# GpSimd waits for the landing of a group of indirect transfers before it issues the next group, in four stages of a graph network

## What is computed

```python
# layer 0: gated edge messages, then a norm over the graph
msg = silu(h[src] + (edge_attr @ we.T + be)); agg = segment_sum(msg, dst)
# layer 1: one softmax over all edges, messages summed by src
e = leaky_relu(h[src] @ a_src + h[dst] @ a_dst + a_b); att = softmax(e, axis=0)
out = segment_sum(att * h[dst], src)
# layer 2: eight heads, softmax over the edges of a node
score = clip(K[src] . Q[dst] / 4, -5, 5); out = segment_sum(softmax_dst(score) * V[src], dst)
# layer 3: an MLP over [x[src], x[dst], edge_attr], summed by dst, then an MLP over nodes
rel = mlp(concat(x[src], x[dst], edge_attr)); out = mlp(concat(x, segment_sum(rel, dst)))
```

## Time and profile before

| | |
|---|---|
| median of 3 runs | 6226.86 us (6226.12 to 6229.10) |
| profiled execution, first to last instruction | 6321.6 us |
| busy: PE, DVE, ACT, POOL | 67%, 47%, 26%, 54% of the span |
| conv, GpSimd's first to last gather | 88.5 to 1351.4 us |
| place | 1514.7 to 2881.2 us |
| heads | 3237.0 to 4619.6 us |
| relation | 4691.2 to 6161.0 us |

### The profile page before, as it was taken

One profiled execution on the slowest core, in us unless ns is written; L12 is line 12 of the kernel. 1 busy time (PEld: TensorE's weight loads), 2 busy tenths in 40 slices (PEclk: granted clock), 3 DMA queues, 4 the chain that ended last, 5 costly groups with the idle time before them and its releaser, 6 DMA issues. The chain is left out here.

```text
span 6321.6 us, 91693 instructions
## 1 busy us (share of the span) xinstructions
PE 4256.0 (67%) x19917; PEld 3740.8 (59%) x19918; DVE 2983.7 (47%) x8050; ACT 1666.9 (26%) x2996; POOL 3424.5 (54%) x3536
## 2 busy tenths in 40 slices
PE   3555555556777777787855555555568888888887
PEld 3444544445766777776744445445456666667765
DVE  5444444456332333235755555555564444444445
ACT  0111111113222222226732222222233333333331
POOL 3655655532566656566635556555525555555550
PEclk6666566666555555558976666666679999998999
DMA  4233323234222222225733333333334444444441
GB/s 103 81 83 83 83 78 82 80 71 109 78 80 80 80 80 81 79 77 169 206 99 99 100 97 101 99 101 97 98 105 131 132 131 133 128 128 132 133 128 48
DMA packets 491156, 645.54 MB, mean 102 GB/s; under 512 B 94519, under 2 KB 354059, under 8 KB 490798
## 3 DMA queue, kind: packets, MB, share of 16 engines
q0 software_dynamic: 132032, 325.99, 18.1%
q1 hardware_dynamic: 346462, 312.02, 17.6%
q10 hardware_dynamic: 12560, 6.52, 0.6%
HBM read 554.38 MB, written 89.82 MB: 102 GB/s over the span
## 5 line engine op out<-in xcount | busy, mean ns | idle before, releaser
L1610 POOL DMA_INDIRECT R<-table_ps,r_idx x832 | 809.6, 973 | 731.9 <-DVE r_idx L1684 417.5
L1195 POOL DMA_INDIRECT by_src<-R,p_idx x832 | 826.3, 993 | 627.9 <-issue 246.0
L1390 POOL DMA_INDIRECT R<-table_kv,h_idx x832 | 805.3, 968 | 647.7 <-issue 324.3
L660 POOL DMA_INDIRECT R<-table,c_idx x784 | 750.5, 957 | 548.5 <-issue 307.7
L1420 PE MATMUL psum<-R,h_oh 128*128 128x137 f32 x1664 | 405.0, 415 | 627.8 <-issue 291.4
L693 PE MATMUL psum<-R,c_oh 128*128 x1664 | 380.1, 400 | 620.4 <-DVE R L752 375.0
L1420 PEld LDWEIGHTS psum<-R,h_oh 128*128 128x128 f32 x1664 | 344.2, 295 | 679.8 <-issue 494.5
L693 PEld LDWEIGHTS psum<-R,c_oh 128*128 128x128 f32 x1664 | 324.3, 290 | 673.5 <-issue 673.5
L1632 PE MATMUL psum<-w_L_gnn_re_w,r_ea 128*128 128x256 f32 x1664 | 555.3, 417 | 226.5 <-DVE X L1724 209.7
L1745 DVE TENSOR_TENSOR R<-R,psum 128x256 f32 x832 | 346.9, 417 | 752.0 <-remote 344.6
L1008 PE MATMUL psum<-R 128*128 x1664 | 428.5, 424 | 189.0 <-issue 187.0
(11 more groups left out here) (339 smaller groups left out, 7696.9 us busy)
## 6 DMA issues: line engine op xcount, KB each, us to landing
R<-by_src SPq DMA_DIRECT2D x220, 260.0 KB, 3.1
r_ea<-in_ea_t SPq DMA_DIRECT2D x832, 64.0 KB
R<-in_ea_t SPq DMA_DIRECT2D x196, 256.0 KB
R<-rel_rows SPq DMA_DIRECT2D x104, 256.0 KB
R<-lo_rows SPq DMA_DIRECT2D x104, 256.0 KB
h_rel<-rel_rows SPq DMA_DIRECT2D x208, 128.0 KB
r_rel<-rel_rows SPq DMA_DIRECT2D x208, 128.0 KB
by_src<-R,p_idx POOLq DMA_INDIRECT x832
```

Source lines behind the costliest of these rows:

```text
L660: g.indirect_dma_start(out=rows[:, u, :], out_offset=None, in_=table, in_offset=bass.IndirectOffsetOnAxis(ap=idx[:, j // GROUPS % 2, u:u + ...
L1195: g.indirect_dma_start(out=by_src, out_offset=bass.IndirectOffsetOnAxis(ap=idx[:, u:u + 1], axis=0), in_=rows[:, u, :], in_offset=None).th ...
L1390: g.indirect_dma_start(out=rows[:, u, :], out_offset=None, in_=table, in_offset=bass.IndirectOffsetOnAxis(ap=idx[:, u:u + 1], axis=0)).the ...
L1610: g.indirect_dma_start(out=rows[:, u, :], out_offset=None, in_=table, in_offset=bass.IndirectOffsetOnAxis(ap=idx[:, u:u + 1], axis=0)).the ...
```

## The change

GpSimd gets one more wait before it begins a group of four transfers: for the semaphore of the last transfer of the preceding group. In conv this holds for every group but the very first; in place, heads and relation for the second, third and fourth group of each iteration (`if u:`), not for the first. In conv the first 16 groups are now written out ahead of the loop (`loads=PER`), so that the loop runs 11 rounds. Nothing else is changed: the same transfers, slots and waits of the other engines.

```diff
--- before.py
+++ after.py
@@ -654,6 +654,10 @@
                     if j % GROUPS == 0:
                         g.wait_ge(idx_ready, TURNS * i + j // GROUPS + 1)
                     g.wait_ge(row_free, PER * i + j + 1)
+                    if not (isinstance(i, int) and i == 0 and j == 0):
+                        before_j = (j - 1) % GROUPS
+                        turn = TURNS * i + j // GROUPS + (1 if j % GROUPS else 0)
+                        g.wait_ge(row_in[G * before_j + G - 1], 16 * turn)
                     g.sem_inc(pool_turn, 1)
                     for q in range(G):
                         u = G * (j % GROUPS) + q
@@ -661,7 +665,7 @@
                                              in_offset=bass.IndirectOffsetOnAxis(ap=idx[:, j // GROUPS % 2, u:u + 1], axis=0)
                                              ).then_inc(row_in[u], 16)
 
-                staggered(g, PER, (gather, 0, TILE_GROUPS))
+                staggered(g, PER, (gather, 0, TILE_GROUPS), loads=PER)
 
             @block.tensor
             def _(pe):
@@ -1191,6 +1195,8 @@
                             g.wait_ge(ready, n + 1)
                         if u % G == 0:
                             g.wait_ge(rows_ready, 2 * n + u % G8 // G + 1 + 2 * PER)
+                            if u:
+                                g.wait_ge(row_out[u - 1], 16 * i + 16)
                             g.sem_inc(pool_turn, 1)
                         g.indirect_dma_start(out=by_src, out_offset=bass.IndirectOffsetOnAxis(ap=idx[:, u:u + 1], axis=0),
                                              in_=rows[:, u, :], in_offset=None).then_inc(row_out[u], 16)
@@ -1386,6 +1392,8 @@
                         if u % G == 0:
                             g.wait_ge(idx_ready, GROUPS * i + u // G + 1)
                             g.wait_ge(msg_ready, GROUPS * i + u // G + 1)
+                            if u:
+                                g.wait_ge(row_in[u - 1], 16 * i + 16 * (before + 1))
                             g.sem_inc(pool_turn, 1)
                         g.indirect_dma_start(out=rows[:, u, :], out_offset=None, in_=table,
                                              in_offset=bass.IndirectOffsetOnAxis(ap=idx[:, u:u + 1], axis=0)
```

## The result

The changed kernel takes **6829.75 us** (median of four runs, 6828.59 to 6839.71) against 6226.49 (6223.87 to 6229.10): a ratio of 1.0965 [1.0941, 1.0990], or +603 us. The forecast was +343, and the time lies above the range. The sign is as predicted, and so is conv as the stage that loses most; the size is not.

What follows compares the result with a forecast made beforehand. No engine is full; GpSimd runs groups ahead, held by VectorE, except in place. Conv +158, heads +59, relation +20 and place +110 make +347 us profiled, scaled to +342: 6570 us, range 6390 to 6740.

Steps and rivals of the forecast that it cites:

- the cushion: GpSimd's present idle time per group boundary: 1.72 us in conv, 1.70 in place, 1.88 in heads, 2.29 in relation.
- The restart: At each waited boundary, GpSimd begins 0.84 us after its release, as read from VectorE's message in the timeline.
- The landing: Last packets of each stage's last transfer begin 2.8 us after issue in conv, 1.8 place, 3.1 heads, 3.2 relation.
- Conv: Gap 2.6 us at 195 boundaries, group 7.33 us against 6.45, GpSimd becomes the bound: +158 us.
- Place: Gap 2.1 us, iteration 26.1 against 26.3, but boundaries without lead make ScalarE late: +110 us, between none and 179.
- Heads: Gap 2.8 us at three of four boundaries, iteration 27.8 us against 26.6: +59 us.
- The base: Terms summed on the profiled 6321.6 us, 1.5% above the median 6226.86, then scaled in proportion: +347 becomes +342 us.
- Relation: Gap 2.8 us, iteration 27.9 against 28.3, fits on average; scattering iterations cost +20 us, bounded by 0 and 130.
- The long gap: Rival: gap 3.1 us in all stages and place pays in full, 6907 us; chance 0.12.
- The short gap: Rival: gap 2.1 us in all stages, conv +60, place +60, heads and relation fit, 6347 us; chance 0.10.
- The wait is met: Rival: thresholds count too low, the wait is met when reached, nothing changes, 6227 us; chance 0.02.
- the level case: Rival: gap 1.7 us everywhere, GpSimd stays ahead in conv, 6215 to 6240 us; chance 0.04.

Runs made afterwards that it cites:

- e11: Wait in conv alone, SyncE's load held back until GpSimd begins its next group, against the kernel before: 6486.17 us, ratio 1.0199.
- e2: The new wait in place alone, the other stages as before, against the kernel before: 6366.35 us, ratio 1.0231.
- e13: The three waits in place alone, SyncE's loads there tied to GpSimd's groups, against the kernel before: 6234.04 us, ratio 1.0019.
- e14: The waits in heads alone, SyncE's load per group there tied to a group's start, against the kernel before: 6348.28 us, ratio 1.0189.
- e4: The new wait in relation alone, the other stages as before, against the kernel before: 6201.84 us, ratio 0.9974.
- e7: Wait in conv alone, but for the last gather of the group two back, against the kernel before: 5154.30 us, ratio 1.0004.
- e9: The whole change run again in the third session, against the kernel before (6365.78 us there): 6834.44 us, ratio 1.0736.
- e15: The whole change run again in the fourth session, against the kernel before (6224.20 us there): 6816.44 us, ratio 1.0940.
- e12: Wait in place alone, only the one between the halves of an iteration, against the kernel before: 6351.16 us, ratio 0.9974.

## Why the prediction was right in sign and wrong in size

**What bounds the kernel, and the cushion.** Right: GpSimd became the bound in conv and heads as forecast, and the cushion of 1.7 to 2.3 us per boundary, summed over an iteration, is what the gaps had to exceed. It did so in place too, where the forecast took the floor (26.1) to be level with the pace.

**The restart, 0.84 us.** About right: 0.76 us in conv and relation, 0.79 in place and 0.86 in heads, from the rise of the semaphore to the next transfer.

**The landing: the step that failed.** The prediction read it from "the last transfer of each stage, behind which nothing is queued". That is one landing per stage, and not in the case that the change makes the rule. The wait puts the readers, and through their buffers SyncE's loads, in step with the landing, so that in conv and at two of three boundaries in place a 256 KB load nearly always runs beside the very transfer that is waited for. Measured landings are 3.0 us in conv (2.8 taken, by when packets begin; another 0.35 until the semaphore is seen to rise was left out) and 3.4, 1.9 and 3.0 in place (1.8 taken, and the gap raised to 2.1). Moving the loads brings place's gap to 2.23, so its 2.1 was a good figure for an undisturbed scatter. Conv's 2.6 was not: an undisturbed gather gives 2.4. The gather that it was read from was itself a slow one. The packets that raise its semaphore are 4 bytes each and don't show in the slices; the last of them began 4.0 us after the issue, against 2.2 us for those of e11. So a single last transfer was no measure either way. The three terms:

- *Conv*, 2.6 forecast, 3.2 measured: 195 x 0.6 = 117 us. The message after runs from 96.2 to 1643.6, before from 96.0 to 1367.1: +276, which is the forecast's 158 and this 117.

```profile
L756 DVE TENSOR_TENSOR R<-psum,R x196: 680/692/693, 96.2 to 1643.6; 128x512 f32<-128x512 f32 x196
its engine sat idle before it (us, times) until:
  DMA R<-table,c_idx: 389.5, 185
```

- *Place*, 2.1 forecast, 3.16 measured: the floor of an iteration rises to 29.3 us, three above today's, and the stage pays 3.0 x 52 = 156 (e2: +144 in time). The +110 rested on another ground, boundaries without slack that make ScalarE late. ScalarE does wait for scatters now, 1015.9 us in 89 waits where it had 423.3 on what the profile calls remote; but that is GpSimd being the bound seen from ScalarE: in e13 it still waits for scatters for 668.2 us in 65 waits, and the time is up by 12 us only.

```profile
ACT R L1051 <- DMA by_src<-R,p_idx: 1015.9, 89, 13.4
```

- *Heads*, 2.8 forecast. The waits view of GpSimd lists all three boundaries of each iteration, after and then in e14:

```profile
POOL R L1398 <- DMA R<-table_kv,h_idx: 452.0, 156, 4.1
```

```profile
POOL R L1395 <- DMA R<-table_kv,h_idx: 410.5, 156, 3.4
```

  452.0 / 156 = 2.90 us, and 2.63 with the loads moved. Some 20 us for the gap; the transfers also keep GpSimd for 999 ns instead of 968, 832 x 0.031 = 26 us, which the forecast held constant.

**The base.** The sum was made against the profiled execution and scaled by 0.985 as a whole. That execution was slow mainly in heads (26.6 us per iteration; 25.3 to 25.7 in four traces of the same code where before takes 6226 us) and a little in conv. With GpSimd as the bound a stage's end doesn't depend on how slow it was before, so the cost of the wait has to be counted from the median's pace: some 55 us more in heads, some 20 in conv. These terms against the misses: in conv 117 + 20 = 137 for 131, in heads 20 + 26 + 55 = 101 for 91, in place 156 - 110 = 46 for 36. They were found after the fact, and what is left is within the intervals of the single runs.

**Relation.** The gap is as forecast (2.78 and 2.8), and so is the fit: 27.5 us per iteration against 28.3 in the profile of before. The price of 20 us, bounded by 130, for iterations that scatter didn't come; the stage took 1431.7 us, as much as it takes without the wait (1429.7 in e2, 1436.9 in e14), and e4 was 16 us faster.

**The rivals.** The long gap was the nearest for the wrong reason: its 3.1 us is what conv, place and heads show, but it put relation's straggler there and had place pay for 105 boundaries at 2.7 us. The short gap is what e11 and e13 come near, only with the loads moved. "The wait is met" is refuted by the waits above, the level case by every gap. What the Trainium skill says of a lighter HBM load, page DMA: Bandwidth & Descriptors, section "Latency and other measured facts", did not decide here: DMA's share fell from 0.30 to 0.25 in conv, and the landing was 3.0 us all the same.

**Clock and arithmetic.** Both rightly costed at nothing: the clock fell by 0.04 in conv, where TensorE is busy for 725 of 1551 us, and e7 has conv's arithmetic at 1.0004.

## What to carry to other kernels

A wait on a landing doesn't only add the landing's time: it brings everything that hangs on the same landing into step, other queues' loads among it, so take the landing's price with these loads beside it, or move them. When the wait makes an engine the bound, price the stage by that engine's own cycle (4 transfers, their spacing and the gap), and set it against the pace of several executions, not of the profiled one alone. If a wait is needed, one on an earlier transfer (in conv two groups back: free; the third of four: a gap of 1.2 us and not of 3.2) keeps more of the lead.

## What the runs showed of the hardware that was not expected

**The same kernel before took 5155, 6226 or 6366 us in different sessions, and the stages with the wait took the same.** In the slower sessions TensorE and SyncE have spells in which an instruction takes some 0.7 us to issue. Counted from the records of place, 102 to 155 matmuls start 0.6 to 0.8 us after the one before in kernels without a felt wait there, and 24 to 31 in the session of 5155; of SyncE's 2117 issues of a DMA 185 to 310 take over 0.6 us in the slower sessions, and 20 or 21 in that one. What causes them is open.

**Pacing GpSimd takes most of TensorE's away in the same stage.** With the wait in place (after, e2, e9, e13, e15) 22 to 25 such matmuls are left there; in relation 13 to 39 become 6 to 10. One line of the page shows it, TensorE's second product of the expansion in place (line 1008 before). In turn: before, with 189.0 us of idle time just ahead; e12, whose wait is hardly felt; e2; after; and e7, without a wait in place but in the session of 5155:

```profile
L1008 PE MATMUL psum<-R 128*128 x1664 | 428.5, 424 | 189.0 <-issue 187.0
```

```profile
L1008 PE MATMUL psum<-R 128*128 x1664 | 415.3, 424 | 156.0 <-issue 155.2
```

```profile
L1008 PE MATMUL psum<-R 128*128 x1664 | 382.8, 423 | 0.0
```

```profile
L1012 PE MATMUL psum<-R 128*128 x1664 | 382.5, 423 | 0.1
```

```profile
L1012 PE MATMUL psum<-R 128*128 x1664 | 381.1, 422 | 0.0
```

It may be the source of e4's 16 us, but that is not shown: relation itself, 1429.4 us in e4, is no shorter than in e2 without the wait (1429.7), and no run held GpSimd back by something other than a landing.
